# Selective scan block: four C products by way of TensorE and ScalarE, and two sets of layer-norm statistics on ScalarE

## What is computed

```
h = layernorm(x) * (1 + ca) + sa
x_dbl = h @ x_proj_w.T ;  dt, B, C = split(x_dbl, [128, 16, 16])
delta = softplus(dt @ dt_proj_w.T + dt_proj_b) ;  A = -exp(A_log)
for t in tokens:                       # state s is (256 channels, 16)
    s = exp(delta[t, :, None] * A) * s + delta[t, :, None] * B[t] * h[t, :, None]
    y[t] = sum_n s[:, n] * C[t, n] + D * h[t]
x = x + ga * y
```

## Time and profile before

| | us |
|---|---|
| median of 3 runs | 301.56 (297.92 to 303.89) |
| the profiled execution | 297.89 |
| its span, first to last instruction | 296.1 |
| VectorE busy | 263.8 |
| TensorE busy | 249.2 |
| GpSimd busy | 226.8 |
| ScalarE busy | 191.1 |
| mean granted clock of TensorE | 0.872 |

### The profile page before, as it was taken

The page is one execution under the profiler, slowest core; times in us unless marked ns, Lnnn a source line. Parts: engine busy times, 40 slices in busy tenths (PEclk is TensorE's granted clock), DMA queues, the critical chain, the costliest instruction groups (busy, mean ns, idle before and its releaser), DMA issues.

```text
span 296.1 us, 3901 instructions
## 1 busy us (share of the span) xinstructions
PE 249.2 (84%) x1250; PEld 188.0 (63%) x1250; DVE 263.8 (89%) x346; ACT 191.1 (65%) x310; POOL 226.8 (77%) x113
## 2 busy tenths in 40 slices
PE   7866389689976996687599999975799997999994
PEld 7624276379865565464496767653778776787762
DVE  4579998799998989999999999989999999987761
ACT  2597756785574695797645976793347498444650
POOL 1005799999999999998998999799869999960000
PEclk9995559977557699996979999997599997999999
DMA  7906899548436164468251465571566640001102
GB/s 243 363 20 178 151 145 240 90 71 246 120 87 129 40 143 107 100 97 131 34 128 54 126 158 105 114 151 35 159 167 202 154 127 0 2 0 35 35 2 75
DMA packets 34437, 33.81 MB, mean 114 GB/s; under 512 B 14960, under 2 KB 21488, under 8 KB 34416
## 3 DMA queue, kind: packets, MB, share of 16 engines
q1 hardware_dynamic: 34000, 32.73, 47.1%
q10 hardware_dynamic: 416, 0.81, 0.7%
HBM read 31.12 MB, written 2.36 MB: 113 GB/s over the span
## 4 chain that ended last, share of the span: by engine, by line
POOL 33%; DVE 19%; PE 14%; issue 13%; DMA 10%; ACT 7%; SPq 1%; POOLq 1%; DVEq 0%; ACTq 0%
POOL drv L737 18%; POOL drv L749 12%; DVE state L1212 12%; DMA brow<-bc_dram 6%; DVE drv L1177 4%; DMA ffn_sb<-in_upT 3%; PE sums L1626 2%; PE side L1438 2%; PE side L1549 2%; PE side L1508 2%; DMA resid<-in_x 1%; ACT decay L986 1%; PE rows_ps L1508 1%; POOL u L719 1%; PE side L1525 1%
## 5 line engine op out<-in xcount | busy, mean ns | idle before, releaser
L737 POOL TENSOR_TENSOR drv<-u,brow 128x1024 f32<-128x1024 f32 x63 | 147.8, 2363 | 20.6 <-DVE u L1111 16.8
L986 ACT ACTIVATE decay<-delta,A 128x512 f32<-128x512 f32 x128 | 87.5, 687 | 67.5 <-DVE state L1212 65.8
L1212 DVE TENSOR_TENSOR_SCAN state<-decay,last,drv 128x512 f32<-128x512 f32 x96 | 118.8, 1268 | 2.4 <-ACT decay L986 1.9
L1626 PE MATMUL sums<-ident,drv 128*128 128x128 f32 x504 | 76.9, 309 | 1.6 <-POOL drv L749 1.6
L1626 PEld LDWEIGHTS sums<-ident,drv 128*128 128x128 f32 x504 | 67.7, 162 | 11.8 <-issue 6.6
L749 POOL TENSOR_TENSOR drv<-state,crow 128x1024 f32<-128x1024 f32 x29 | 68.5, 2369 | 2.3 <-DVE state L1212 2.3
L1177 DVE TENSOR_TENSOR drv<-state,rows_ps 128x1024 f32<-128x1024 f32 x34 | 40.7, 1196 | 1.1 <-PE rows_ps L1588 1.1
L1212 DVE TENSOR_TENSOR_SCAN state<-decay,drv 128x512 f32<-128x512 f32 x32 | 37.8, 1209 | 3.5 <-ACT decay L986 3.5
L1588 PE MATMUL rows_ps<-c_parts,sel 64*128 64x512 f32 x35 | 20.2, 577 | 23.5 <-DVE drv L1177 23.3
L1508 PE MATMUL side<-h_hi,ffn_hi 128*128 128x512 f32 x74 | 26.6, 441 | 6.7 <-ACT gates L955 3.3
L1588 PEld LDWEIGHTS rows_ps<-c_parts,sel 64*128 64x128 f32 x35 | 7.4, 211 | 32.5 <-DVE drv L1177 22.1
(11 more groups left out here) (190 smaller groups left out, 335.2 us busy)
## 6 DMA issues: line engine op xcount, KB each, us to landing
brow<-bc_dram SPq DMA_DIRECT2D x31, 512.0 KB, 5.5
crow<-bc_dram SPq DMA_DIRECT2D x13, 512.0 KB, 6.7
resid<-in_x SPq DMA_DIRECT2D x4, 512.0 KB, 5.6
out<-resid SPq DMA_DIRECT2D x8, 256.0 KB, 3.1
gates<-in_wmod ACTq DMA_DIRECT2D x1, 768.0 KB, 5.8
gates<-in_wmod SPq DMA_DIRECT2D x1, 768.0 KB, 8.6
last<-state SPq DMA_DIRECT2D x48, 1.0 KB, 2.9
crow<-bc_dram SPq DMA_DIRECT2D x3, 256.0 KB, 3.7
```

Of the source, the lines that this page charges most:

```text
L737: nc.gpsimd.tensor_tensor(drv[j % RING_DRV][:, :, 0:S], u[:, c % 2, :, 0:S], b.unsqueeze(1).to_broadcast([P, HALVES, S]), ALU.mult).then_i ...
L986: nc.scalar.activation(decay[i % RING_DECAY][:, 0:S], delta[:, c % 2, h, 0:S], ACT.Exp, scale=A[:, h * N + n:h * N + n + 1]).then_inc(deca ...
L1212: nc.vector.tensor_tensor_scan(state[j % RING_STATE][:, h, 0:S], decay[i % RING_DECAY][:, 0:S], drv[j % RING_DRV][:, h, 0:S], before, ALU. ...
L1626: ins = nc.tensor.matmul(sums[:, b * D + h * P:b * D + (h + 1) * P], of[:, h, b * P:(b + 1) * P], ident[:, :], is_transpose=True, start=Fa ...
```

## The change

- **Turned products.** `TURN_C` names four products (states 8 and 10 of chunk 0, 0 of chunk 1, 0 of chunk 2) that take another way. TensorE transposes the state, two token blocks at a time, into `rows_ps` (`turn`: four transposes of 128x128 a half). There tokens lie on partitions, so C[t, n] is a column, and ScalarE multiplies by it (`times_c` of ScalarE, two operations of 128x256 a half) into `drv`. The second half uses the same bank after the first is read. TensorE adds the result with four products of 128x256 with the identity. For this C itself is turned once for chunks 0, 1 and 2 ("F cT").
- **Who makes the rest.** Product 6 of chunk 0 and product 9 of chunk 1 move from GpSimd to VectorE. GpSimd has 27 products (29), VectorE 33 (35).
- **Statistics.** For the first layer norm of chunks 2 and 3 (`BY_SCALAR`) VectorE's statistics go. ScalarE makes a sum (a copy with accumulator) and a sum of squared deviations (a square with a bias and accumulator) for each of four token blocks, and the mean between them. For chunk 2 they stand in slots 12.5 to 14 of chunk 0, for chunk 3 in slots 1 to 4 of chunk 1.

```diff
-POOL_C = [[4, 6, 9, 11, 13]] + [[1, 3, 5, 7, 9, 10, 13]] * (NCH - 3) + [[1, 3, 5, 6, 7, 10, 13]] + [[1, 2, 4, 5, 7, 10, 11, 12, 13, 14]]
+POOL_C = [[4, 9, 11, 13], [1, 3, 5, 7, 10, 13], [1, 3, 5, 6, 7, 10, 13], [1, 2, 4, 5, 7, 10, 11, 12, 13, 14]]
+TURN_C = [[8, 10], [0], [0], []]
...
-DVE_C = [[n for n in range(N) if n not in at] for at in POOL_C]
+DVE_C = [[n for n in range(N) if n not in at and n not in turned] for at, turned in zip(POOL_C, TURN_C)]
...
     "scalar": [
+        (16, "F cT"),
...
+        (-3.5, "F sum0.2"), (-3, "F sum1.2"), (-3, "F mean.2"), (-2.5, "F dev0.2"), (-2, "F dev1.2"),
+        (-15, "F sum0.3"), (-14.5, "F sum1.3"), (-14.5, "F mean.3"), (-14, "F dev0.3"), (-12, "F dev1.3"),
...
+BY_SCALAR = (2, 3)
+SECOND_LATER = {"st0": -7, "st1": -7, "agg": 3, "rstd": 2.5, "nmr": 3, "cT": -1}
...
+TURN_LAG = 1
...
+                if kind == "F" and plan is PLAN and (name in ("st0", "st1", "agg") and chunk in BY_SCALAR or
+                                                     name[:3] in ("sum", "mea", "dev") and int(name[-1]) != chunk):
+                    continue
...
+                elif name[:3] in ("sum", "dev"):
+                    q, dev = int(name[3]), name[:3] == "dev"
+                    act.wait_ge(x_loaded[c], 16)
+                    if dev:
+                        act.wait_ge(mean_ready, BY_SCALAR.index(c) + 1)
+                    for b in range(2 * q, 2 * q + 2):
+                        unread, of = xn["K"][:, b, :], resid[:, BLK0[c] + b, :]
+                        if dev:
+                            ins = nc.scalar.activation(unread, of, ACT.Square, bias=negmean[kind][:, b:b + 1],
+                                                       accum_out=sum_sq[:, b:b + 1])
+                        else:
+                            ins = nc.scalar.activation(unread, of, ACT.Copy, accum_out=sum_x[:, b:b + 1])
+                    ins.then_inc(dev_ready if dev else sum_ready, 1)
...
+            def times_c(c, n, q):
+                j = c * N + n
+                act.wait_ge(turned, 2 * turns(c, n) + q + 1)
+                for b in range(2):
+                    to = flat(drv[j % RING_DRV])[:, (2 * q + b) * D:(2 * q + b + 1) * D]
+                    ins = nc.scalar.activation(to, rows_ps[:, b * D:(b + 1) * D], ACT.Copy,
+                                               scale=cT[:, c % 2, 2 * q + b, N + n:N + n + 1])
+                ins.then_inc(prod_act, 1)
...
                     for task in side_tasks("scalar", step, n):
                         side_work(*task)
+                    for c, m in turned_at(step, n, TURN_LAG + 1):
+                        times_c(c, m, 0)
                     if scanning:
                         make_decay(step, n, 1)
                     for task in side_tasks("scalar", step, n + 0.5):
                         side_work(*task)
+                    for c, m in turned_at(step, n, TURN_LAG + 1):
+                        times_c(c, m, 1)
...
+                if turns_upto(c, n):
+                    pe.wait_ge(prod_act, 2 * turns_upto(c, n))
...
+            def turn(c, n, q):
+                j, rows = c * N + n, rows_upto(c) + len([m for m in DVE_C[c] if m < n])
+                if q == 0:
+                    if rows:
+                        pe.wait_ge(prod_dve, rows)
+                    if turns(c, n):
+                        pe.wait_ge(prod_act, 2 * turns(c, n))
+                    pe.wait_ge(scan_done, upto_scan(c, n, HALVES - 1))
+                else:
+                    pe.wait_ge(prod_act, 2 * turns(c, n) + 1)
+                for b in range(2):
+                    for h in range(HALVES):
+                        ins = nc.tensor.transpose(rows_ps[:, b * D + h * P:b * D + (h + 1) * P],
+                                                  state[j % RING_STATE][:, h, (2 * q + b) * P:(2 * q + b + 1) * P],
+                                                  ident[:, :])
+                ins.then_inc(turned, 1)
...
+                if n in TURN_C[c]:
+                    for b in range(NBLK[c]):
+                        ins = nc.tensor.matmul(sums[:, b * D:(b + 1) * D], ident[:, :], flat(of)[:, b * D:(b + 1) * D],
+                                               start=False, stop=False)
...
+                    for c, m in turned_at(step, n, TURN_LAG):
+                        turn(c, m, 0)
+                    for c, m in turned_at(step, n, TURN_LAG + 1):
+                        turn(c, m, 1)
```

More of the change, by code:

```diff
@@ L261, in side_tasks, with turns, turns_upto, turned_at @@
                 yield kind, name, int(chunk)
+def turns(c, n):
+    return sum(map(len, TURN_C[:c])) + TURN_C[c].index(n)
+def turns_upto(c, n):
+    return sum(len([m for m in TURN_C[b] if (b, m) < (c, n)]) for b in range(c + 1))
+def turned_at(step, slot, lag):
+    return [(c, n) for c, n in lagged(step, slot, lag) if n in TURN_C[c]]
 def product_slot(c, n):
@@ L446, in adaln_block @@
         added = sem("added")
+        turned = sem("turned")
+        prod_act = sem("prod_act")
+        cT_ready = sem("cT_ready")
         half_made = sem("half_made")
@@ L846, in side_work @@
                         act.wait_ge(eps_ready, 1)
+                    if kind == "F" and c in BY_SCALAR:
+                        act.wait_ge(dev_ready, NPAIR[c] * (BY_SCALAR.index(c) + 1))
+                        nc.scalar.activation(logvar[kind][:, 0:nb], sum_sq[:, 0:nb], ACT.Ln, scale=1.0 / D, bias=eps[:, :])\
+                          .then_inc(logvar_ready[kind], 1)
+                        act.wait_ge(logvar_ready[kind], c + 1)
+                        nc.scalar.activation(rstd[kind][:, 0:nb], logvar[kind][:, 0:nb], ACT.Exp, scale=-0.5)\
+                          .then_inc(rstd_ready[kind], 1)
+                        return
                     act.wait_ge(meanvar_ready[kind], c + 1)
@@ L863, in side_work @@
                       .then_inc(rstd_ready[kind], 1)
+                elif name[:3] in ("sum", "dev"):
[11 more added lines that the diff above has]
+                    ins.then_inc(dev_ready if dev else sum_ready, 1)
+                elif name[:4] == "mean":
+                    act.wait_ge(sum_ready, NPAIR[c] * (BY_SCALAR.index(c) + 1))
+                    act.wait_ge(nmr_ready[kind], c)
+                    nc.scalar.activation(negmean[kind][:, 0:nb], sum_x[:, 0:nb], ACT.Copy, scale=-1.0 / D)\
+                      .then_inc(mean_ready, 1)
                 elif name[:2] == "xn":
@@ L1208, in scan @@
                             dve.wait_ge(*upto_prod(cb, nb_))
+                        if nb_ in TURN_C[cb]:
+                            dve.wait_ge(turned, 2 * (turns(cb, nb_) + 1))
                         if cb < NCH - 1:
@@ L1478, in side_work @@
                     product(("F bc", c, 0), S, 2 * N, lambda k: xbc_sb[:, k, :], lambda k: hmod[:, c % 2, k, 0:S])
+                elif name == "cT":
+                    pe.wait_ge(bc_ready, c + 1)
+                    to, full = take(("F cT", c, 0))
+                    for b in range(nb):
+                        ins = nc.tensor.transpose(to[:, b * 2 * N:(b + 1) * 2 * N], bc_sb[:, b * P:(b + 1) * P],
+                                                  ident[0:2 * N, 0:2 * N])
+                    ins.then_inc(full, 1)
                 elif name in ("z", "z0", "z1"):
```

28 lines of the change are left out of this document (24 added, 4 removed), and 8 rows, old and new, of tables (FIRST, PLACE, PLAN).

## The result

| | before | after |
|---|---|---|
| median of 6 runs each, same chip | 299.51 us (297.92 to 303.89) | 303.19 us (301.63 to 305.19) |
| ratio, 95% interval | | 1.0107 [1.0062, 1.0152] |
| the profiled execution, its span | 297.89, 296.1 | 302.12, 300.3 |
| mean granted clock in it | 0.872 | 0.897 |

The changed kernel is about 1% slower, where I had forecast 1.7 us less than before. Medians are over all runs of a kernel, while the ratio and its interval leave out runs that were over 1.5% above the fastest of the same kernel, so that the two can differ, by up to 0.9% in the table further down.

What follows compares the result with a forecast made beforehand. VectorE was taken to set the pace, with GpSimd beside it and ScalarE's decays just in time. Terms -1.5 + 1.1 - 0.75 - 0.6 = -1.75, say -1.7, gave 299.9 us against the median 301.56; range 294.5 to 304.5.

Steps and rivals of the forecast that it cites:

- The copies of C: Three small copies on ScalarE, booked only within its added work of about 15.5 us, with no wait.
- walk of chunk 0: Slot-by-slot reckoning of chunk 0 from slot 7: product 14 starts at about 81.0, 1.3 us late.
- Identity products: On TensorE, four of 128x256 at 0.24 us each were to equal the eight transposed adds they replace.
- Pairs: Two ScalarE multiplications of 128x256 for a turned product: 0.85 us a pair, bounds 0.8 to 1.4.
- Scan (13,0): Chunk 0, VectorE: starts at 72.8 instead of 71.39, with ScalarE idle for the load of x before it.
- the first rival: ScalarE's work fits between the decays in 55 to 80; VectorE's full -5.5 us comes through, 296.0; chance 0.25.
- The boundary: Chunk 0 to 1: GpSimd's product 13 is 2.3 us earlier, so the resid add starts at 89.8, not 91.28: -1.5.
- Product with W: Chunk 1, TensorE: starts at about 95.0 and runs at the high clock, 3.67 us, so the whole -1.5 stays.
- the rival that had it low: The low clock stays at the product with W in chunk 1 (6.53 us): 1.1 us worse, 301.0; chance 0.15.
- Product 9 on VectorE: Chunk 1: moved from GpSimd, nothing hides it, +1.1 us.
- Product 0 of chunk 2: Leaves VectorE: at best -1.1 us, half booked, -0.6, since the resid add hangs on 24 adds only just in time.
- slower than before: Rival: the x load holds chunk 0's decays longer, product 14 is 5.2 us late, +3.4, 305.0; chance 0.18.

Runs made afterwards that it cites:

- e_copy_only: The kernel before plus only an unused turned copy of C of chunk 0 (TensorE slot 6, ScalarE slot 6.5): 304.28 us, ratio 1.0141.
- g_copy_lateact: The kernel before plus the unused copy of C of chunk 0, transposed in slot 6 but read by ScalarE in slot 8: 299.53 us, ratio 1.0029.
- g_after_lateact: The changed kernel with only ScalarE's read of the turned C of chunk 0 moved from slot 6.5 to 8: 298.03 us, ratio 0.9961.
- b_turn12: The kernel before with only the turned products of state 0 in chunks 1 and 2 added: 299.31 us, ratio 1.0051.
- a_half_id: The changed kernel with identity products of every second token block left out for the four turned products: 301.68 us, ratio 1.0045.
- b_split_only: The kernel before with only product 6 of chunk 0 and product 9 of chunk 1 moved from GpSimd to VectorE: 302.25 us, ratio 0.9975.
- a_no_turn0: The changed kernel with products 8 and 10 of chunk 0 back on VectorE and no copy of C of chunk 0: 302.44 us, ratio 1.0033.
- a_ct_early: The changed kernel with the copy of C of chunk 0 made in slots 2 and 2.5 instead of 6 and 6.5: 298.66 us, ratio 0.9947.
- f_gp_ct: The changed kernel with C of chunk 0 copied in slots 2 and 2.5 and GpSimd's product list as before: 296.08 us, ratio 0.9887.
- a_no_stats: The changed kernel with the statistics of chunks 2 and 3 back on VectorE: 303.49 us, ratio 1.0140.
- g_best: The changed kernel with C of chunk 0 copied in slots 2 and 2.5, GpSimd's list as before, x loads in slot 8: 298.46 us, ratio 0.9977.

## Why the prediction was wrong, step by step

My sum was made of differences against the profiled execution, so I set each term against the same differences in the two traces.

- **The copies of C: the step that failed.** The walk of chunk 0 has product 14 at 1.3 us late; it was 5.15 late (84.82 for 79.67), and the whole error of chunk 0 is made before it. The prediction puts "three small copies of C" into ScalarE's added 15.5 us, and the walk of chunk 0 starts at slot 7 without them. The price of the copy, 0.28 us, was never the question. I did not ask what TensorE has to finish before the four transposes, or which decay stands behind the copy. I gave its wait nothing, without a reason; it was 1.59 us in the trace. Its place costs 4.7 us by itself (e_copy_only), and nothing when the read is 1.5 slots later (g_copy_lateact). In the earlier trace rows the same product with W took 3.67 us even at the high clock; that is how long a transpose behind it has to wait.
- **Identity products, mis-sized by half.** I counted 10 records in 2.43 us as ten products. They are five of two records each. Four products are eight records (the 16 products of after have 32) and take 1.97 us at the high clock and 3.45 at the low one, not 0.97; they do not equal eight transposed adds (1.04 in the row at 51.15 above). Leaving half of them out takes 0.9 us from the second jump (3.3 for 4.2) and the whole of a wait in chunk 2 (below); a gain in the medians isn't clear of the intervals.
- **Pairs**: 0.84 and 0.81 for 0.85. Right.
- **Scan (13,0)**: 72.8 forecast, 76.96 found. The mechanism named, a wait for x, is there (0.73 at 72.93) but is not the one that decides: the second turn waits 1.67. In g_after_lateact, where the clock holds, the scan starts at 73.04 and x is waited for 1.17 us, which looks like the walk's figure; but that execution was 1.42 late before the change could act, so the agreement is luck. What the ten traces show is that the walk reckoned with a second turn that is in time, which holds at the high clock and not at the low one.
- **The signs.** Scans waiting for decays 10.5 us, of 7 or more forecast; the first rival (under 4) is out. Resid add at 93.56, not 89.8.
- **The boundary**: I had 2.8 us given back between product 14 and the resid add. Product 14 was 5.15 late and the add 2.28, so 2.87 came back. Right. In sum chunk 0 and the boundary gave **+2.3** where I had **-1.5**: 3.8 of the 5.9 us by which the sum of differences was off, all of it from the walk of chunk 0.
- **Product with W** in chunk 1: 5.08, between my 3.67 and the 6.53 of the rival that had it low. From 99 to 101 the granted clock was 0.50 and from 101 to 103 it was 0.78. I took the high level, and that was wrong.
- **Not foreseen in chunk 1**: a product waits 1.90 us at 108.11 for its C row, which stands behind the product with W, 16 products for D x h and the 1.89 us of identity products (before 1.07): **+0.8**. How much of it is the mis-sized product isn't shown, and the product with W seems to weigh more: in b_turn12, with the same 1.89 us of identity products, W took 3.67 and VectorE didn't wait there at all, while in a_half_id, with 1.03 us of them, W took 6.30 and the wait was 2.36.
- **Product 9 on VectorE**: +1.1 forecast, **+1.14** found (3.09 to 4.23). The same 1.12 or 1.13 in b_split_only, a_no_turn0 (-2.01 to -0.88) and a_ct_early (1.83 to 2.96), and none in f_gp_ct, where GpSimd keeps it (-1.52 and -1.52). This is the surest figure of the case.
- **Statistics of chunk 3**: -0.75 forecast, **-0.75** found (4.23 to 3.48).
- **Product 0 of chunk 2**: -1.14 at once, and +0.86 of it gone again by scan (10,0): **-0.3**, for -0.6. What takes it back is a wait of VectorE for a down product that comes late on TensorE (the row under this list). All eleven traces with the turned product and full identity products in chunk 2 have this wait, 0.8 us long. In a_half_id it is gone, and scans (8,0) and (10,0) are equally late. So this part is the mis-sized identity product.
- **Chunk 3 and the end**: 0 forecast, **+1.0** found (3.21 to 4.2); I have no cause to show for it.

```profile
181.18 0.69 DVE L1259 TENSOR_TENSOR resid<-resid,side 128x512 f32<-128x512 f32 x1 [0.79 <-PE side L1667]
```

These are +2.3 +0.8 +1.1 -0.75 -0.3 +1.0 = 4.2, the difference of the spans.

The base was a second, smaller fault. I took the median of the three runs shown, 301.56. Over the 93 runs of before made beside the experiments the median is 300.33. With this base my sum gives 298.6, and the kernel with the read moved, g_after_lateact, is at 298.0. That is near, but its traced parts differ from my terms, so I don't call it a proof of the sum.

Of the rivals, "slower than before" had 0.18 with 305.0: the right side and about the right size (303.2). It even has product 14 at 5.2 us late, and it was 5.15; but its cause, the load of x, is refuted by a_no_stats, so this is luck.

What stays open is by which way a wait of 1.6 us comes to cost 4.7: a part is the wait itself (1.56 by scan (8,0) in e_copy_only), the rest comes later, while the clock is low in that trace, and no experiment separates the two. The low level doesn't need the wait: in the profiled executions of a_ct_early and g_best, which have no such wait, 60 to 76 stood at 0.79 and scan (14,0) was 2.7 and 3.0 late. The mean clock over the runs was 0.853 in e_copy_only against 0.865 in before beside it, and 0.879 in g_copy_lateact against 0.872, so the copy's place seems to change how often or how long the clock is low, not whether it can be.

## What to carry to other kernels

A step is priced by what it waits for and by what is queued behind it, before it is priced by its duration: for each new instruction on an engine that must deliver just in time, write down the producer's whole queue in front of it. Where an engine that must deliver just in time reads what another engine makes, put the read a slot or more later than looks necessary; for the copy of C it cost nothing and was worth 5.2 us (for the turned products themselves it wasn't tried). An fp32 product is to be counted in records when its price is taken from a grouped row.

## What the runs showed of the chip

- **Within one kernel the time goes with TensorE's clock.** Over the 93 runs of before the time falls with the mean granted clock by 1.35 us for 0.01 (correlation -0.80, and -0.79 or stronger on each of the four chips): from 295.66 us at 0.893 to 304.57 at 0.846. VectorE has the largest share of busy time here, and yet the time goes with TensorE's clock. Which of the two drives the other isn't shown, and between kernels it doesn't hold: after has the higher clock and the longer time. The three runs that I took for a base had a median of 301.56, the six of the comparison 299.51.
- **TensorE can stay at 1.2 GHz for long while it is busy**: 60 to 92 all at 0.50 in e_copy_only, with TensorE busy 15.0 and 16.0 of each 16 us. In the 4 us ahead of that, 56 to 60, it was busy 1.81. That doesn't explain it by itself: in before it was busy 1.52 of the same 4 us, and there the clock was low only for a part of 60 to 64 (0.57) and back at 1.00 from 64 to 68.
- **An fp32 product of 128x256 with the identity** takes 0.49 us at the high clock and 0.86 at the low one (1.97 and 3.45 for four), a transpose of 128x128 about 0.13 at the high clock (eight in 1.04) and 0.24 at the low one (eight in 1.95 at 81.95 in a_half_id).
- **ScalarE's accumulator read** is 0.19 us, but two passes of 128x256 with their reads start only 0.42 us apart (72.93 and 73.35 in after, where a pass takes 0.42 and 0.40): nearly all of the read lies beside the passes.
